# Layer 3's causal mask for the row maximum: added by VectorE in the operation that takes the maximum, in place of a matmul into the score bank

## The chip, the cores and the metric

One core of a Trainium2 chip runs the whole program. The metric is the device time of one execution in microseconds (us), the median of three runs: 2079.53 us before the change (2074.10 to 2083.88).

## The reference, cut to what matters

Four layers, each `x = x + attention(layernorm(x)) + feed_forward(layernorm(x))`, on 16 sequences of 256 tokens of 128 features. The change is in the attention of the last one:

```python
# layer 3: 16 heads of 8 features, T = 256 tokens
att = einsum('bhtd,bhsd->bhts', q, k) / sqrt(8)
att = att + (alibi + causal)          # causal: -inf where s > t, else 0
att = softmax(att, axis=-1)           # exp(att - max over s), divided by its sum
y = einsum('bhts,bhsd->bhtd', att, v)
x = x + y @ W_proj + b_proj + ffn(xn) # ffn: (silu(xn Wg) * (xn Wu)) Wd
```

The masked entries must not count for the row maximum, nor for the sum.

## The kernel before, in words

Layers are done one after the other. Within a layer the sequences are turns (-2 to 16), and `turn_steps` writes one list of steps a turn that TensorE (PE), VectorE (DVE), ScalarE (ACT) and SyncE (SP) all follow in its order. Turns 2 to 13 are a loop over two turns. Semaphores tie the engines; each instruction stream is in program order.

Attention of layer 3 needs two score matrices a head. In step S (`row_scores`, lines 531 to 541) a head's scores lie with queries on the partitions: queries 0 to 127 against keys 0 to 127 in bank columns 0 to 127, and queries 128 to 255 against all 256 keys in columns 128 to 383. DVE takes the two maxima from the bank (lines 1236 and 1237) into `mx`. In step M the maxima of 8 heads are transposed by PE (line 664) and subtracted from the extra rows of `stk` by DVE (line 1245), so that the second score matrix comes with the maximum taken off. In step T (`key_scores`, line 555) the scores are made again with keys on the partitions, ACT takes the exponential (line 804) and step O multiplies by the values (line 694).

Step S is one sequence ahead of step T. The list has T0 S1 H0 T1 S0 T2 S3 O3 M1 T3 S2 T4 S5 H1 J0 T5 S4 J1 T6 S7 O0 P0 T7 S6 Q0 P1 T8 S9 H2 Q1 V0 T9 S8 V1 T10 S11 O1 W0 M0 T11 S10 T12 S13 Y0 T13 S12 T14 S15 O2 T15 S14. (H and Y: the feed forward; J: divide by the sum; P and V: queries, keys and values of a later sequence; Q and W: the output projection.) Where a T is followed by an S, PE issues them as a pair: mask of T, waits for S's bank and operands, mask of S, then the four score matmuls (lines 665 to 674). The masks are matmuls of an identity with a bf16 mask (line 546 for T, line 528 for S), which start the bank with -1e30 above the diagonal; the scores are accumulated on them.

The steps S, M, P, V and J share the two banks of `pS` in turn: PE starts a use when DVE has freed the bank two uses before (`S_free`). Operands of S come from DRAM: SP stores the sequence that step W finished (line 1437, after a wait for W's vector operation), then packs queries and keys into DRAM with three transfers (line 1401), waits until they have landed, and spreads them over the partitions with one transfer for heads 0 to 7 and one for heads 8 to 15 (line 1412). S1 of the next turn waits for the first of these.

`tc.link` (line 239 is its wait) makes DVE wait for its own last operation; `settle` (line 224) is a semaphore increment of the engine by itself, with nothing waiting for it.

Of the kernel before, what the change touches and what calls it, by code (L numbers as in the profile page):

```python
# [17 lines left out]
BF16 = mybir.dt.bfloat16  # L18
I32 = mybir.dt.int32
U32 = mybir.dt.uint32  # L20
ALU = mybir.AluOpType
# [200 lines left out]
def settle(eng, sem):  # L222

    eng.sem_inc(sem, 1)
# [47 lines left out]
def build(nc, d, out):  # L272
    ctx = ExitStack()
    with ctx:
# [8 lines left out]
        def sem(name):  # L283
            if name not in sems:
# [55 lines left out]
        ident = sb("ident", [P, P])  # L340
        onesr = sb("onesr", [1, P])
        onesm = sb("onesm", [P, P])
        maskb = sb("maskb", [P, 2, P], BF16)
        identb = sb("identb", [P, P], BF16)
        rank = sb("rank", [P, NT, 16])
        neghalf = sb("neghalf", [P, NT])
# [63 lines left out]
            "ld_0": [(wr[0][:, :], d["wr0"]), (wq0[:, :, :], d["wq0"]), (bq0[:, :], d["bq0"]),  # L410
                     (bv0[:, :], d["bv0"].partition_broadcast(P))],
            "ld_cst": [(onesr[:, :], d["c_ones"][0:1, :]), (onesm[:, :], d["c_ones"]),
                       (maskb[:, :, :], d["c_mask"]), (identb[:, :], d["c_identb"]), (rank[:, :, :], d["c_rank"]),
                       (tri[:, :], d["c_tri"]), (rope0[:, :, :], d["c_rope0"]),
                       (rope2[:, :, :], d["c_rope2"]), (bitf[:, :], d["c_bitf"]), (blockno[:, :], d["c_blockno"])],
            "ld_1": [(wr[1][:, :], d["wr1"]), (br[1][:, :], d["br1"].partition_broadcast(P)),
# [54 lines left out]
        def _(pe):  # L471
# [50 lines left out]
            def head_rows(h):  # L522
                return slice(32 * (h % NG), 32 * (h % NG) + 32), h // NG

            def row_scores_mask(l, bank):

                if l == 3:
                    pe.matmul(bank.rearrange("p (c n) -> p c n", c=2)[:, :, 0:P], identb[:, :],
                              maskb[:, 0, None, :].to_broadcast([P, 2, P]), start=True, stop=True)

            def row_scores(l, side, h, bank, part):

                rows, j = head_rows(h)
                if l == 3:
                    c = 1 - part
                    o = bank[:, P:P + T] if c else bank[:, 0:P]
                    return pe.matmul(o, stk[rows, side, j, c * P:(c + 1) * P],  # L537
                                     stk[rows, side, j, T:T + (c + 1) * P],
                                     start=False, stop=True, skip_group_check=True)
                return pe.matmul(bank[:, part * T:(part + 1) * T], stk[rows, side, j, part * P:(part + 1) * P],  # L540
                                 stk[rows, side, j, T:2 * T], start=True, stop=True)

            def key_scores_mask(l, bank):

                if l == 3:
                    pe.matmul(bank.rearrange("p (c n) -> p c n", c=2)[:, :, 0:P], identb[:, :],
                              maskb[:, 1, None, :].to_broadcast([P, 2, P]), start=True, stop=True)

            def key_scores(l, side, h, bank, part):

# [9 lines left out]
            def take_turn(turn):  # L560
# [4 lines left out]
                for at, (kind, k, local) in enumerate(turn.steps):  # L565
# [73 lines left out]
                    elif kind == "P":  # L639
                        w = {0: wq0, 2: wq2, 3: wq3}[l]  # L640
                        for n, which in enumerate({0: [2 * k, 2 * k + 1]}.get(l, [k])):
                            ins = pe.matmul(bank[:, n * T:(n + 1) * T], w[:, which, :],  # L642
                                            XT[:, bass.ts(turn.row(2), T)], start=True, stop=True)
                        ins.then_inc(s("S_full"), 1)
                    elif kind == "V":
                        pe.wait_ge(s("row_staged"), PRIMED + turn.row(2))
                        w = {0: wq0[:, 4, :], 2: wq2[:, 2, :], 3: wq3[:, 2, :]}[l]
                        pe.matmul(bank[:, 0:P], xtb[:, nxt, k * P:(k + 1) * P], w, start=True, stop=True)\
                          .then_inc(s("S_full"), 1)
                    elif kind == "S":  # L650
                        if not paired:
                            pe.wait_ge(s("S_free"), PRIMED + use_s + local - 1)
                            row_scores_mask(l, bank)
                        pe.wait_ge(s(f"spread{k // 8}"), PRIMED + turn.count(16, 32))
                        if not paired:
                            row_scores(l, nxt, k, bank, 0)
                        row_scores(l, nxt, k, bank, 1).then_inc(s("S_full"), 1)
                        paired = False
                    elif kind == "M":

                        last = max(loc for kd, kk, loc in turn.steps[:at] if kd == "S") if k == 0 else -1
                        pe.wait_ge(s("S_free"), PRIMED + use_s + last + 1)
                        for n in range(4):
                            ins = pe.transpose(bank[:, n * P:(n + 1) * P], mx[:, n % 2, 2 * k + n // 2, :], ident[:, :])  # L664
                        ins.then_inc(s("S_full"), 1)
                    elif kind == "T":
                        if k < 8:
                            pe.wait_ge(s("S_free"), PRIMED + use_s - uses_behind_maxima(l, turn.n - 1))
                        else:
                            pe.wait_ge(s("S_free"), PRIMED + use_s + used_at(turn, "M", 1) + 1)  # L670
                        key_scores_mask(l, bank)
                        after = turn.steps[at + 1]
                        paired = after[0] == "S"
                        if paired:
                            other = pS[:, turn.s_bank(after[2]), :]
                            pe.wait_ge(s("S_free"), PRIMED + use_s + after[2] - 1)
                            pe.wait_ge(s(f"spread{after[1] // 8}"), PRIMED + turn.count(16, 32))
                            row_scores_mask(l, other)
                        key_scores(l, par, k, bank, 0)
                        if paired:  # L680
                            row_scores(l, nxt, after[1], other, 0)
                        key_scores(l, par, k, bank, 1).then_inc(s("T_full"), 1)
                    elif kind == "O":

                        back = 1 if k == NJ - 1 else 0
                        made = 0 if back else used_at(turn, "T", NG * k + NG - 1) + 1
                        pe.wait_ge(s("T_free"), PRIMED + use_t + made)
                        pe.wait_ge(s("v_ready"), PRIMED + turn.row(1 - back))
                        pe.wait_ge(s("O_free"), PRIMED + use_o + local)
                        for kc in range(2):  # L690
                            q0 = P if l == 3 and kc == 1 else 0
                            for g in range(NG):
                                h = NG * k + g
                                ins = pe.matmul(pO[32 * g:32 * g + DH + 1, q0:T],  # L694
                                                va[:, par ^ back, kc, h, :],
                                                pex[:, h % 8, kc * T:kc * T + T - q0],
                                                start=(kc == 0), stop=(kc == 1))
                        ins.then_inc(s("O_full"), 1)
                    elif kind == "J":

                        copied = [loc for kd, kk, loc in turn.steps if kd == "O" and kk == NJ - 1][0]
                        pe.wait_ge(s("O_free"), PRIMED + use_o + copied + 1)
                        for j in range(NJ):
                            ins = pe.transpose(bank[:, j * P:(j + 1) * P], oTf[:, j, k * P:(k + 1) * P], ident[:, :])
                        ins.then_inc(s("S_full"), 1)
                    elif kind == "Q":
                        pe.wait_ge(s("out_read"), PRIMED + turn.row())
                        pe.transpose(bank[:, 0:P], ob[:, k, :], ident[:, :]).then_inc(s("T_full"), 1)
                    elif kind == "W":
                        turned = [loc for kd, kk, loc in turn.steps if kd == "Q" and kk == 1][0]  # L710
                        pe.wait_ge(s("T_free"), PRIMED + use_t + turned + 1)
                        for c in range(2):
                            ins = pe.matmul(yb[:, c * P:(c + 1) * P], oT[:, c * P:(c + 1) * P], wp3[:, :],
                                            start=True, stop=True)
                        ins.then_inc(s("Y_full"), 1)
# [229 lines left out]
        def _(dve):  # L945
# [224 lines left out]
            def take_turn(turn, tc):  # L1170
# [17 lines left out]
                for kind, k, local in turn.steps:  # L1188
# [44 lines left out]
                    elif kind == "S":  # L1233
                        j, col = k // NG, 32 * (k % NG) + MAXROW
                        if l == 3:
                            dve.tensor_reduce(mx[:, 0, j, col:col + 1], bank[:, 0:P], AX.X, ALU.max)  # L1236
                            ins = dve.tensor_reduce(mx[:, 1, j, col:col + 1], bank[:, P:P + T], AX.X, ALU.max)  # L1237
                        else:
                            ins = dve.tensor_reduce(mx[:, :, j, col], bank.rearrange("p (c n) -> p c n", c=2),  # L1239
                                                    AX.X, ALU.max)  # L1240
# [225 lines left out]
def shape_constants():  # L1466
# [14 lines left out]
    fixed[:, 1, 1, 0], fixed[:, 1, 1, 1] = np.arange(T) / 256.0, -slope  # L1481
    c["c_fixed"] = fixed.reshape(P, 2, 2 * T)
    m = np.where(np.arange(P)[None, :] > np.arange(P)[:, None], -1e30, 0.0).astype(f)
    c["c_mask"] = np.stack([m, m.T], axis=1)
    c["c_identb"] = np.eye(P, dtype=f)
    freqs = (f(1.0) / np.power(f(10000.0), np.arange(0, DH, 2, dtype=f) / f(DH))).astype(f)
    ang = np.arange(T, dtype=f)[:, None] * freqs[None, :]
# [69 lines left out]
```

## Time and profile before

| | us |
|---|---|
| median of 3 runs | 2079.53 |
| the profiled execution, its own time | 2077.18 |
| its span | 2074.8 |
| layer 3's first maximum to the last | 1636.9 to 2047.8 |
| PE busy, whole span | 1624.0 |
| DVE busy, whole span | 1238.6 |
| ACT busy, whole span | 766.0 |

Times in the rows are us from the start of the span; a busy share is that of an engine whose instructions overlap at their ends. The granted clock (PEclk) is 1.00 for 2.4 GHz and 0.50 for 1.2 GHz.

### The profile page before, as it was taken

Reading aid. Unit: us, or ns where it says so; the run is one execution under the profiler, and the core shown is the slowest. Engines: PE = TensorE matmul, PEld = TensorE weight load, DVE = VectorE, ACT = ScalarE, POOL = GpSimd, SP = SyncE. Lnnn points to the kernel's source line nnn. Section 1 sums busy time; section 2 is a strip of 40 time slices with the busy share of each in tenths; the row PEclk is TensorE's granted clock in tenths of the full one; section 3 lists DMA queues with packets and bytes.
Section 4 is the critical chain, followed back from the end, with each engine's and each line's share of the span. In section 5 each row is a group of like instructions: output and inputs, shape, how many; then the busy total and the mean of one; then the engine's idle time right before and its main releaser. Section 6 shows DMA issues by size and latency. Waiting matters only on the chain.

```text
span 2074.8 us, 44343 instructions
## 1 busy us (share of the span) xinstructions
PE 1624.0 (78%) x12567; PEld 1050.6 (51%) x12567; DVE 1238.6 (60%) x3512; ACT 766.0 (37%) x1723; POOL 380.3 (18%) x488
## 2 busy tenths in 40 slices
PE   3257999999972599998983588888887688888888
PEld 3123666666632577877872244444543344444444
DVE  6454666566675665665574455555557566666664
ACT  2013445445441222322230254445454144434444
POOL 1274101101167011111123300000006200000000
PEclk9855999999965698988885598999997599999999
DMA  7023455455421000000001332333232111111110
GB/s 233 28 70 101 141 155 174 137 157 174 130 58 37 0 1 1 0 0 0 0 1 40 89 95 89 98 112 110 82 95 57 36 39 42 40 40 39 37 40 15
DMA packets 133278, 144.90 MB, mean 70 GB/s; under 512 B 15001, under 2 KB 114130, under 8 KB 132946
## 3 DMA queue, kind: packets, MB, share of 16 engines
q1 hardware_dynamic: 127058, 131.37, 21.4%
q0 software_dynamic: 6144, 12.60, 2.1%
q8 instruction: 38, 0.62, 0.1%
q14 instruction: 38, 0.31, 0.0%
HBM read 104.65 MB, written 39.52 MB: 69 GB/s over the span
## 4 chain that ended last, share of the span: by engine, by line
PE 48%; DVE 19%; issue 13%; DMA 8%; POOL 7%; SPq 2%; ACT 2%; DVEq 1%; ACTq 0%; POOLq 0%
PE pO L694 6%; DMA stk<-packed_qk 6%; PE pT_ L557 5%; PE pH L584 5%; PE pY L592 5%; DVE X L1278 4%; PE pH L500 4%; POOL sorted_x L910 3%; PE pS L642 3%; PE pS L664 3%; DVE mx L1239 2%; PE pT_ L490 2%; PE pY L512 2%; PE pT_ L555 2%; DVE stk L1245 2%
## 5 line engine op out<-in xcount | busy, mean ns | idle before, releaser
L804 ACT ACTIVATE pex<-pT_ 128x512 f32<-128x512 f32 (+1 forms) x768 | 426.6, 562 | 656.1 <-PE pT_ L557 362.8
L1239 DVE TENSOR_REDUCE mx<-pS 128x2 f32<-128x512 f32 x512 | 348.2, 688 | 194.9 <-PE pS L540 176.8
L557 PE MATMUL pT_<-stk 32*128 32x256 f16 x1024 | 208.2, 298 | 120.0 <-DMA stk<-packed_qk 67.0
L540 PE MATMUL pS<-stk 32*128 32x256 f16 x1024 | 220.3, 304 | 23.4 <-DMA stk<-packed_qk 19.6
L694 PE MATMUL pO<-pex,va 128*9 128x256 f32 (+1 forms) x3072 | 218.4, 408 | 2.0 <-ACT pex L804 2.0
L797 ACT ACTIVATE wb<-pH,b 128x256 f32<-128x256 f32 x256 | 107.3, 470 | 268.4 <-PE pH L500 268.4
L883 POOL TENSOR_TENSOR qk<-qkf,qk 128x512 f16<-128x512 f32 x48 | 55.4, 1155 | 779.5 <-DVE qk L1211 407.3
L557 PEld LDWEIGHTS pT_<-stk 32*128 32x128 f16 x1024 | 55.9, 94 | 238.0 <-issue 87.3
L500 PE MATMUL pH<-XT,w 128*128 (+1 forms) x512 | 146.7, 413 | 0.0
L584 PE MATMUL pH<-xsT,wb 128*128 128x128 f32 x888 | 134.1, 297 | 0.0
L1245 DVE SCALAR_TENSOR_TENSOR stk<-pS,stk 128x512 f16<-128x512 f32 x96 | 66.3, 691 | 109.2 <-PE pS L664 105.0
L592 PE MATMUL pY<-wb,hbs 128*128 128x128 f32 x888 | 128.5, 288 | 2.2 <-DVE ysb L1259 2.2
L584 PEld LDWEIGHTS pH<-xsT,wb 128*128 128x128 f32 x888 | 114.6, 202 | 23.2 <-issue 20.8
L807 ACT ACTIVATE xts<-pO 128x256 f32<-128x256 f32 x192 | 73.8, 384 | 130.6 <-PE pO L694 130.6
L592 PEld LDWEIGHTS pY<-wb,hbs 128*128 128x128 f32 x888 | 107.4, 191 | 26.5 <-issue 21.2
L694 PEld LDWEIGHTS pO<-pex,va 128*9 128x9 f32 x3072 | 68.9, 95 | 91.0 <-issue 41.5
L1236 DVE TENSOR_REDUCE mx<-pS 128x1 f32<-128x128 f32 x256 | 73.4, 287 | 60.5 <-PE pS L537 44.7
L642 PE MATMUL pS<-XT,wq 128*128 (+1 forms) x256 | 87.9, 452 | 26.1 <-issue 18.8
L1237 DVE TENSOR_REDUCE mx<-pS 128x1 f32<-128x256 f32 x256 | 105.8, 413 | 0.0
L500 PEld LDWEIGHTS pH<-XT,w 128*128 128x128 f32 x512 | 98.8, 212 | 10.2
L483 PE MATMUL pS<-ident,qkf 128*128 128x128 f32 x128 | 33.0, 429 | 86.9 <-DVE qkf L966 86.9
L910 POOL DMA_INDIRECT sorted_x<-XN,slot x96 | 92.9, 968 | 27.8 <-issue 26.7
(195 smaller groups left out, 2841.5 us busy)
## 6 DMA issues: line engine op xcount, KB each, us to landing
wb<-in_w SPq DMA_DIRECT2D x111, 514.0 KB, 3.8
stk<-packed_qk SPq DMA_DIRECT2D x96, 256.0 KB, 2.8
packed_qk<-qk SPq DMA_DIRECT2D x144, 128.0 KB, 2.0
xsb<-sorted_x SPq DMA_DIRECT2D x111, 64.0 KB, 3.4
sorted_y<-ysb SPq DMA_DIRECT2D x111, 64.0 KB, 3.1
sorted_x<-wb SPq DMA_DIRECT2D x2, 2048.0 KB, 13.3
w<-in_w SPq DMA_DIRECT2D x2, 1024.0 KB
out<-X SPq DMA_DIRECT2D x16, 128.0 KB, 1.8
```

Of the source, the lines that this page charges most:

```text
L500: ins = pe.matmul(bank[:, half * T:(half + 1) * T], w, XT[:, bass.ts(turn.row(), T)], start=True, stop=True)
L540: return pe.matmul(bank[:, part * T:(part + 1) * T], stk[rows, side, j, part * P:(part + 1) * P], stk[rows, side, j, T:2 * T], start=True, ...
L557: return pe.matmul(bank[:, part * T:(part + 1) * T], key, stk[rows, side, j, 0:T], start=True, stop=True)
L584: ins = pe.matmul(pH[:, local % 2, f * P:(f + 1) * P], wb[:, place_, f * P:(f + 1) * P], xsT[:, ring, :], start=True, stop=True)
L592: ins = pe.matmul(pY[:, 0:P], hbs[:, ring, f * P:(f + 1) * P], wb[:, place_, FF + f * P:FF + (f + 1) * P], start=(f == 0), stop=(f == NF - ...
L642: ins = pe.matmul(bank[:, n * T:(n + 1) * T], w[:, which, :], XT[:, bass.ts(turn.row(2), T)], start=True, stop=True)
L694: ins = pe.matmul(pO[32 * g:32 * g + DH + 1, q0:T], va[:, par ^ back, kc, h, :], pex[:, h % 8, kc * T:kc * T + T - q0], start=(kc == 0), s ...
L797: ins = act.activation(hb[:, k % 4, half * T:(half + 1) * T], bank[:, half * T:(half + 1) * T], ACT.Relu, bias=b1[1][:, 2 * k + half:2 * k ...
L804: act.activation(pex[:, k % 8, 0:n], bank[:, 0:n], ACT.Exp).then_inc(s("T_free"), 1)
L910: pool.indirect_dma_start(XS, bass.IndirectOffsetOnAxis(ap=slot[:, choice, t:t + 1], axis=0), XN[:, t, :], None).then_inc(sem("sorted_out" ...
L1239: ins = dve.tensor_reduce(mx[:, :, j, col], bank.rearrange("p (c n) -> p c n", c=2), AX.X, ALU.max)
L1245: dve.scalar_tensor_tensor(q, bank.rearrange("p (j n) -> p j n", j=2), -1.0, q, ALU.mult, ALU.add).then_inc(s("S_free"), 1)
```

## The change: what it does

The 256 mask matmuls of step S are gone (16 heads of 16 sequences); those of step T stay. The scores start their bank themselves. DVE's two maximum operations of a head become two `tensor_tensor_reduce`: each adds the bank (PSUM, f32) and a bf16 mask (SBUF), writes the sum to a new tile `masked` (SBUF, f32, nothing reads it) and writes its maximum to `mx`. Before the first of them stands a `settle`, behind the wait for the scores. The mask is laid out as 512 columns: mask, zeros, mask, and the mask of step T.

```diff
-            def row_scores_mask(l, bank):
-                if l == 3:
-                    pe.matmul(bank.rearrange("p (c n) -> p c n", c=2)[:, :, 0:P], identb[:, :],
-                              maskb[:, 0, None, :].to_broadcast([P, 2, P]), start=True, stop=True)
...
                     return pe.matmul(o, stk[rows, side, j, c * P:(c + 1) * P],
-                                     stk[rows, side, j, T:T + (c + 1) * P],
-                                     start=False, stop=True, skip_group_check=True)
+                                     stk[rows, side, j, T:T + (c + 1) * P], start=True, stop=True)
...
-                            row_scores_mask(l, bank)
...
-                            row_scores_mask(l, other)
...
                         if l == 3:
-                            dve.tensor_reduce(mx[:, 0, j, col:col + 1], bank[:, 0:P], AX.X, ALU.max)
-                            ins = dve.tensor_reduce(mx[:, 1, j, col:col + 1], bank[:, P:P + T], AX.X, ALU.max)
+                            settle(dve, sem("dve_settled"))
+                            for c, at in enumerate((slice(0, P), slice(P, P + T))):
+                                ins = dve.tensor_tensor_reduce(masked[:, turn.s_bank(local), at], bank[:, at],
+                                                               maskb[:, at], 1.0, -3e38, ALU.add, ALU.max,
+                                                               mx[:, c, j, col:col + 1])
...
-        maskb = sb("maskb", [P, 2, P], BF16)
+        maskb = sb("maskb", [P, 4 * P], BF16)
+        masked = sb("masked", [P, 2, 3 * P])
...
-    c["c_mask"] = np.stack([m, m.T], axis=1)
+    c["c_mask"] = np.concatenate([m, np.zeros((P, P), f), m, m.T], axis=1)
```

## Rows read from the trace of the kernel before

**Rows 1.** Stretch, length, busy (count): PE, PEld, DVE, ACT, POOL; clock, DMA, GB/s.

```profile
1863.00:1889.00 26.00, 21.82 (x210) 12.47 (x198) 17.00 (x52) 10.27 (x25) 1.50 (x2) 1.00 0.14 40
```

**Rows 2.** Chain of waits that ended last, one turn (start, length, what).

```profile
1836.31 2.59 DMA stk<-packed_qk
1843.92 0.28 PE pS L528
1848.27 0.28 PE pS L528
1856.05 0.28 PE pS L528
```

**Rows 3.** SP's transfers, timeline of the same turn.

```profile
1833.31 1.36 SPq L1401 DMA_DIRECT2D packed_qk<-qk  x3
1836.31 1.81 SPq L1412 DMA_DIRECT2D stk<-packed_qk  x2
```

**Rows 4.** PE, timeline of the same turn: two pairs of T and S.

```profile
1838.95 0.28 PE L528 MATMUL pS<-maskb,identb 128*128 128x256 bf16 x1 [1.00 <-DMA stk<-packed_qk]
1839.16 0.28 PE L555 MATMUL pT_<-stk 32*128 32x256 f16 x1
...
1840.40 0.27 PE L546 MATMUL pT_<-maskb,identb 128*128 128x256 bf16 x1
1840.51 0.27 PE L528 MATMUL pS<-maskb,identb 128*128 128x256 bf16 x1
```

**Rows 5.** DVE, timeline of the same turn.

```profile
1831.72 0.42 DVE L1332 TENSOR_TENSOR X<-X,pY 128x256 f32 x1 [0.76 <-PE pY L713]
...
1841.01 0.42 DVE L1286 SCALAR_TENSOR_TENSOR hbs<-hbs,pH 128x256 f32<-128x256 f32 x1 [0.82 <-ACT hbs L787]
1841.47 0.42 DVE L1288 SCALAR_TENSOR_TENSOR wb<-hbs,pH 128x256 f32<-128x256 f32 x1
...
1842.01 0.41 DVE L1237 TENSOR_REDUCE mx<-pS 128x1 f32<-128x256 f32 x1
1842.34 0.28 DVE L1236 TENSOR_REDUCE mx<-pS 128x1 f32<-128x128 f32 x1
...
1847.59 0.29 DVE L1236 TENSOR_REDUCE mx<-pS 128x1 f32<-128x128 f32 x1 [0.23 <-DVE ob L1322]
...
1849.76 0.41 DVE L1237 TENSOR_REDUCE mx<-pS 128x1 f32<-128x256 f32 x1
1850.44 0.48 DVE L1214 TENSOR_SCALAR qkf<-pS,bq 128x256 f32<-128x256 f32 x1 [0.27 <-PE pS L642]
...
1858.05 0.42 DVE L1332 TENSOR_TENSOR X<-X,pY 128x256 f32 x1 [0.76 <-PE pY L713]
```

**Rows 6.** Groups of instructions by line and form, 1700 to 1960 us.

```profile
L1237 DVE TENSOR_REDUCE mx<-pS 128x1 f32<-128x256 f32 x156 | 64.4, 413 | 0.0
L1236 DVE TENSOR_REDUCE mx<-pS 128x1 f32<-128x128 f32 x156 | 44.6, 286 | 34.9 <-PE pS L537 24.3 <-DVE ob L1322 2.3 <-DVE X L1328 2.2
...
L1223 DVE TENSOR_TENSOR va<-pS,bv 128x128 f32<-128x128 f32 x18 | 5.0, 281 | 0.0
...
L1269 DVE TENSOR_TENSOR X<-X,pY 128x256 f32 x9 | 3.8, 422 | 9.1 <-PE pY L518 9.1
```

**Rows 7.** DVE in layer 1: timeline, and two groups of tiny operations.

```profile
801.13 0.49 DVE L1299 BATCH_NORM_STATS2 zs<-pS 128x6 f32<-128x128 f32 x2 [2.57 <-PE pS L637]
801.77 0.25 DVE L1303 BATCH_NORM_AGGREGATE zmv<-zs 128x2 f32<-128x6 f32 x2
...
L1303 DVE BATCH_NORM_AGGREGATE zmv<-zs 128x2 f32<-128x6 f32 x26 | 3.2, 165 | 1.9
...
L1363 DVE TENSOR_SCALAR lam<-lamt 128x1 f32<-128x1 f32 x1 | 0.2, 154 | 0.2 <-DVE GA L1011 0.2
```

**Rows 8.** DVE, timeline of the first turn with S steps: every second head.

```profile
1638.44 0.29 DVE L1236 TENSOR_REDUCE mx<-pS 128x1 f32<-128x128 f32 x1 [0.17 <-PE pS L537]
...
1639.97 0.29 DVE L1236 TENSOR_REDUCE mx<-pS 128x1 f32<-128x128 f32 x1 [0.17 <-PE pS L537]
```

More of the change, by code:

```diff
@@ L412, in build @@
             "ld_cst": [(onesr[:, :], d["c_ones"][0:1, :]), (onesm[:, :], d["c_ones"]),
-                       (maskb[:, :, :], d["c_mask"]), (identb[:, :], d["c_identb"]), (rank[:, :, :], d["c_rank"]),
+                       (maskb[:, :], d["c_mask"]), (identb[:, :], d["c_identb"]), (rank[:, :, :], d["c_rank"]),
                        (tri[:, :], d["c_tri"]), (rope0[:, :, :], d["c_rope0"]),
@@ L546, in key_scores_mask @@
                     pe.matmul(bank.rearrange("p (c n) -> p c n", c=2)[:, :, 0:P], identb[:, :],
-                              maskb[:, 1, None, :].to_broadcast([P, 2, P]), start=True, stop=True)
+                              maskb[:, None, 3 * P:4 * P].to_broadcast([P, 2, P]), start=True, stop=True)
             def key_scores(l, side, h, bank, part):
```

## The prediction, made before the changed kernel was run

> **What bounds the kernel now.** I read the busy time by stretch first. W's vector operation comes every 26.33 us (1831.72, 1858.05 [rows 5]), which is a turn of layer 3; in 26.00 us of it PE is busy 21.82 us, DVE 17.00 us and ACT 10.27 us, at the full clock (1.00) [rows 1]. No engine is full, so the turn must be a loop of hand-overs, and I went to the chain of waits, then to the timelines of SP, PE and DVE. Two parts close the loop. I cut them at the transfer that brings heads 0 to 7.
>
> Part B is a chain of transfers. Step W's vector operation starts at 1831.72 and ends at 1832.14 [rows 5]; SP stores, then packs from 1833.31, and spreads at 1836.31, when the packed rows have landed [rows 3]; that spread lands at 1838.90 [rows 2], and S1 starts at once, after PE has idled 1.00 us for it [rows 4]. Fixed: 6.8 us from W's end, whatever PE and DVE do in it. Five of the 16 heads (T11 to T15 with their S) run in its shadow.
>
> Part A runs from there (1838.95) to the next W (1858.05) [rows 4, 5], 19.1 us with the other 11 heads. PE's order sets most of it, but PE hands to DVE and back. The chain of waits goes through S mask matmuls at 1843.92, 1848.27 and 1856.05, which waited for DVE to free a bank [rows 2]; what freed it were maxima and M's vector operation. So the same head's step is on the path both as PE's mask and as DVE's maximum. The reader is to see that a saving counts only in part A, and that the change takes from PE and gives to DVE inside one loop.
>
> **What is removed.** Where PE only follows its order, a mask costs the step from L546 to L528, 1840.40 to 1840.51: 0.11 us. Where PE waits for a bank or a transfer ahead of it, the mask of T has long run, and what goes is the whole step from L528 to the scores, 1838.95 to 1839.16: 0.21 us [rows 4]. In part A the path goes through four masks of the second kind (1838.95, and the three of the chain) and one of the first (T8 with S9, behind P1): 4 x 0.21 + 0.11 = 0.95 us a turn. The other masks of part A are beside work of DVE or ACT that ends later; they are worth nothing unless that work shrinks. Those of part B only lengthen PE's idle 1.00 us. Over the span 256 masks at 0.11 us would be 28 us of PE; I count about half of that on the path.
>
> **What is added, per head.** I call the growth of DVE's pair of operations a.
> - The streams. A two-source operation on PSUM takes 281 ns for 128 columns and 422 ns for 256, against 286 and 413 ns for the maxima [rows 6]. Growth: 0.00 to 0.01 us; I take none. The extra output `masked` goes to SBUF with nobody waiting.
> - The maximum as a second output. No operation of this trace has two outputs. From below: it rides along, and a is 0.01. From above: each becomes a tiny operation of its own that starts only when the main one has ended: that loses the overlap of about 0.08 us (a maximum starts at 1842.34, 0.33 us behind one of 0.41 [rows 5]) and adds one of 154 ns [rows 7], so 0.23 each, a = 0.46. Between: a tiny operation queued directly behind. Two aggregations of 128x2 take 0.25 us together and one 0.165 [rows 7], so the second adds 0.085; twice, a = 0.17. I take 0.17, since these are the rows of a tiny result behind another operation with no wait.
> - The Trainium skill, "VectorE: DVE Perf Modes", section "Two Vector instructions with no wait between them", says that an operation that also writes out its accumulator is two instructions, the main one and an accumulator read. No run here shows it yet. It speaks against the change, and for the middle or upper bound. By the 75 ns per overlapped instruction in its "Vector Engine (DVE) Microarchitecture Reference" (5.2), a would be an estimated 0.15.
> - The settle, s. Behind a wait for its own statistics and a settle, DVE's aggregation starts at 801.77, 0.15 us after 801.62 [rows 7]; a maximum after a plain own wait and one increment (1847.59) shows 0.23 us of idle [rows 5]. A bare own wait takes about 0.04 (1841.43 to 1841.47 [rows 5]). So one more increment is about 0.12 us where DVE is idle or has just waited for itself, and none where it is busy with another operation and the increment passes meanwhile. The sequencer does run ahead: maxima follow each other at 0.33 us [rows 5]. Bounds 0 and 0.15; I take 0.12 for heads S4, S7 and S8, which stand behind own waits of J0, J1 and V0, and 0 for S0 and S6. What is queued behind the settle on DVE is the rest of the list, J, P, V and M among it, and PE waits for these by `S_free`.
>
> **The sum for part A.** Shift of each hand-over against before, in us:
> - S1's scores -0.21; H0, S0's maximum and M1 follow: -0.21 + a. Mask of S5 gone behind M's vector operation: -0.42 + a. H1 and J0 likewise. S4: -0.42 + 2a + s.
> - Two ways to P0's vector operation. Through PE (S7's scores without mask, O0, P0): -0.63 + 2a + s. Through DVE (J1, S7's maximum): S7's maximum ends at about 1850.09 in overlap terms (1849.76 + 0.33) and P0 starts at 1850.44 [rows 5]: 0.35 us, of which 0.03 is a hand-over and 0.32 slack: -0.42 - 0.32 + 3a + 2s = -0.74 + 3a + 2s.
> - With a = 0.17, s = 0.12 these are -0.17 and +0.01; DVE is the later: +0.01. P1 waits for P0: +0.01. T8 with S9: -0.10. H2, V0 the same. S8: -0.10 + 0.17 + 0.12 = +0.19. S11's scores without mask: -0.02. O1, W: -0.02.
>
> In closed form the turn moves by -0.70 + 4a (at s = 0.12), zero at a = 0.175: the gain of PE and the price of DVE cancel. In part B DVE has 5 x (0.17 + 0.12) = 1.45 us more, but its waits there are for PE, and PE has the idle 1.00 us and 5 x 0.11 of masks: hidden. If that cover went, each further 0.1 us would be 0.1 a turn. S and T steps overlap in turns 0 to 14: 15 x -0.02 = -0.3 us.
>
> The first turn has S without T. Two heads take 1.53 us there (1638.44 to 1639.97), 0.77 each, PE-paced: DVE idles 0.17 us before each second head [rows 8]. Without the mask DVE paces, at its pair's 0.54 us (286 and 413 ns [rows 6], each less the overlap of 0.08) + 0.17 = 0.71: -0.06 over perhaps 10 heads, -0.6 us; with settles exposed, +0.5. I take 0. Layers 0 to 2 are untouched; the mask's load, 512 columns in place of 256, lies among the loads of the start, far ahead of layer 3.
>
> Sum: 2077.2 - 0.3 = 2076.9 us against the profiled execution's 2077.18. The median of the runs shown is 2.35 us above that, so I forecast 2079.
>
> **The rivals.** Half a per cent of the time, 10.4 us, is about what a measurement of this kernel tells from none.
> - Slow result (slower). The maximum is written by an operation that waits for the main one's end. Place: S0, S4, S7 and S8 of part A, between DVE and PE. Decides from a = 0.345. At a = 0.46: -0.70 + 1.84 = +1.14 us a turn, +17 us: 2097; at a = 0.35, 2090. For: nothing in the trace writes two results. Against: small operations overlap. Chance 0.23.
> - Free result (faster). a = 0.01: -0.66 us a turn, -10 us: 2069; with the settle hidden as well (s = 0) -1.0, -15 us: 2064. For: the vector engine has gaps of 9 us a turn, and the sequencer runs ahead. Against: the settle follows own waits. Chance 0.14.
> - Half rate (slower). An operation with two sources and two results goes one column in two clocks: 384 columns more at the rate of 128 in 0.127 us (413 - 286 ns [rows 6]) are 0.38 us, a = 0.55 with the tiny results: +1.5 a turn, 2102. The Trainium skill's "Vector Engine (DVE) Microarchitecture Reference" (section 7) has such halving for two SBUF sources that are not bf16; here one is PSUM and the other bf16, so by it none is due. Chance 0.06.
> - That the masks were not on the path at all (the change does for PE nothing that counts): then only DVE's side is left, 2a to 4a a turn less what slack takes, +5 to +10 us: 2087. The chain of waits speaks against it. Chance 0.07.
>
> The forecast (a from 0.10 to 0.30, 2073 to 2087 us) has 0.50. **Numbers.** Faster by over 0.5% takes 0.12 (most of the free result), slower 0.23 (the slow result above 2090, half rate), within 0.5% the rest, 0.65. The range is 2068 to 2097: from the free result to the slow one at a = 0.46.
>
> **What would show it.** Lines 528's groups gone and PE's busy time down by 256 x 0.28 us in the records; scores directly behind T's mask at about 0.2 us; after a wait, at once. On DVE two operations of about 0.29 and 0.42 us a head and perhaps two tiny ones; the start of the next operation behind the pair 0.17 us later than now; 0.34 in place of 0.23 us of idle behind J and V. PE's idle time for the spread at the turn's start should grow from 1.00 to about 1.5 us, and the period of the turns stay at 26.3 to 26.5 us. Wrong would be a period off by 0.3 us or more, a pair of over 1 us, or PE's wait for the spread shrinking to nothing, which would mean that DVE paces part B too.

## The result and the profile after

| | before | changed |
|---|---|---|
| median of 4 runs, us | 2078.12 | 2097.82 |
| the profiled execution, its own time | 2077.18 | 2093.68 |
| layer 3, first maximum to last | 1636.9 to 2047.8 | 1633.8 to 2064.7 |

Ratio of the changed kernel to the one before: 1.010, 95% interval 1.0053 to 1.0148. In a second comparison (e5) it was 1.0134 (1.0069 to 1.0199). Slower, by about 20 us, and 20 us is what layer 3 is longer by in the profile (410.9 to 430.8 us). The prediction said 2079, range 2068 to 2097.

The operations first, in the groups by line and form of the changed kernel, 1700 to 1960 us (they answer to [rows 6]):

```profile
L1230 DVE CUSTOM_DVE_ANT_0 masked<-pS,maskb 128x256 f32<-128x256 f32 x150 | 62.9, 419 | 0.0
L1230 DVE CUSTOM_DVE_ANT_0 masked<-pS,maskb 128x128 f32<-128x128 f32 x150 | 43.1, 287 | 37.9 <-PE pS L532 25.5 <-DVE va L1215 3.5 <-DVE ob L1317 3.5
...
L1230 DVE DVE_READ_ACCUMULATOR2_ANT mx<- 128x1 f32 x300 | 24.8, 83 | 0.1
```

The main operations take 287 and 419 ns, where the plain maxima took 286 and 413. Each has a second, tiny instruction that reads the accumulator, 83 ns. What it costs its engine shows in the timeline of VectorE, changed kernel (it answers to [rows 5]):

```profile
1829.94 0.29 DVE L1230 CUSTOM_DVE_ANT_0 masked<-pS,maskb 128x128 f32<-128x128 f32 x1 [0.38 <-DVE ob L1317]
...
1844.69 0.42 DVE L1230 CUSTOM_DVE_ANT_0 masked<-pS,maskb 128x256 f32<-128x256 f32 x1
1845.04 0.08 DVE L1230 DVE_READ_ACCUMULATOR2_ANT mx<- 128x1 f32 x1
1845.04 0.28 DVE L1230 CUSTOM_DVE_ANT_0 masked<-pS,maskb 128x128 f32<-128x128 f32 x1
1845.25 0.08 DVE L1230 DVE_READ_ACCUMULATOR2_ANT mx<- 128x1 f32 x1
1845.25 0.42 DVE L1230 CUSTOM_DVE_ANT_0 masked<-pS,maskb 128x256 f32<-128x256 f32 x1
```

The read and the next main operation start together (1845.04, 1845.25). Behind the operation of 256 columns the next one starts after 0.35 us, where it was 0.33. So a, the growth of a head's pair of operations, is 0.02 to 0.03 us, not 0.17. The first operation behind a wait of VectorE for its own last one starts after 0.38 us of idle, where it was 0.23: 0.15 more.

So VectorE's side came out cheap, and the kernel is slower all the same. The busy time by stretch, from the store of turn 0 to that of turn 13 (13 turns), tells why. Each row gives the stretch, its length, the busy time (and count) of PE, PEld, DVE, ACT and POOL, the mean granted clock and the DMA share and rate; before above, changed below:

```profile
1697.60:2042.10 344.50, 292.07 (x2780) 165.93 (x2779) 226.95 (x685) 141.22 (x325) 17.95 (x24) 1.00 0.14 40
```

```profile
1696.50:2059.40 362.90, 297.86 (x2574) 166.12 (x2570) 231.92 (x1101) 141.12 (x325) 17.95 (x24) 0.87 0.13 38
```

PE has 206 matmuls fewer and is busy for longer, since its mean granted clock is 0.87 in place of 1.00. The clock has two levels in these rows, 0.50 (1.2 GHz) and 1.00 (2.4 GHz), so 0.87 means 0.13 x 2 x 362.9 = 94 us at the low one. The trace's own records of the clock say 92 us, and 3.4 us for the kernel before. A piece of a low stretch in turn 0, in which PE has no idle time at all, and then four whole turns from store to store, changed kernel:

```profile
1708.00:1712.00 4.00, 4.00 (x31) 1.67 (x31) 2.60 (x11) 1.51 (x4) 0.00 (x0) 0.50 0.00 0
...
1841.01:1866.99 25.98, 20.06 (x199) 11.50 (x198) 17.84 (x86) 10.83 (x25) 1.50 (x2) 1.00 0.14 40
1759.48:1786.10 26.62, 22.74 (x205) 13.03 (x203) 18.05 (x86) 10.83 (x26) 1.50 (x2) 0.90 0.14 40
2004.65:2030.18 25.53, 20.13 (x202) 11.51 (x198) 17.91 (x85) 10.87 (x25) 1.50 (x2) 1.00 0.14 41
1730.63:1759.48 28.85, 23.65 (x199) 13.19 (x198) 17.98 (x85) 10.88 (x25) 1.50 (x2) 0.85 0.13 38
```

The turns at 1.00 take 25.98 and 25.53 us; the one at 0.85 takes 28.85. A turn of the kernel before:

```profile
1832.57:1858.84 26.27, 22.35 (x216) 12.77 (x214) 17.50 (x54) 10.86 (x25) 1.50 (x2) 1.00 0.14 40
```

Against the same turns before (26.28 and 26.09 us) the change is a gain of 0.3 to 0.6 us a turn where the clock is full. At full clock PE is now busy 20.1 us of a turn, where it was 22.4. PE's timeline, changed kernel, shows the start of a low stretch, which the clock's records put at 1792.07, for 6.8 us:

```profile
1790.65 0.28 PE L540 MATMUL pT_<-maskb,identb 128*128 128x256 bf16 x1
1792.52 0.39 PE L549 MATMUL pT_<-stk 32*128 32x256 f16 x1 [1.59 <-DMA stk<-packed_qk]
...
1792.95 2.08 PE L501 MATMUL pH<-XT,wf 128*128 x4
```

PE waits 1.59 us for the spread (1.00 before [rows 4]; I had said 1.5). The clock falls within this wait, and the four matmuls that follow take 2.08 us. In the kernel before the same four took 1.13:

```profile
1839.43 1.13 PE L500 MATMUL pH<-XT,wf 128*128 x4
```

### The profile page after: what moved, and what is told of

It reads as the page before. It is cut to its first block, busy times and chain, and to the rows that moved or that the text cites. A ratio compares the mean times of both kernels' runs of the same rounds, so it can differ in the third digit from the quotient of the medians.

```text
span 2091.6 us, 44614 instructions
## 1 busy us (share of the span) xinstructions
PE 1631.5 (78%) x12311; PEld 1049.9 (50%) x12311; DVE 1244.1 (59%) x4024; ACT 766.2 (37%) x1723; POOL 381.2 (18%) x488
## 4 chain that ended last, share of the span: by engine, by line
PE 48%; DVE 19%; issue 14%; DMA 7%; POOL 7%; SPq 2%; ACT 1%; DVEq 1%; ACTq 0%; POOLq 0%
PE pO L686 6%; PE pT_ L551 5%; PE pH L578 5%; DMA stk<-packed_qk 5%; PE pY L586 5%; PE pH L501 5%; DVE X L1273 4%; POOL sorted_x L902 3%; PE pS L657 3%; PE pS L636 3%; DVE mx L1234 3%; PE pT_ L549 2%; PE pT_ L491 2%; PE pY L513 2%; POOL XN L922 1%
## 5 line engine op out<-in xcount | busy, mean ns | idle before, releaser
L686 PE MATMUL pO<-pex,va 128*9 128x256 f32 (+1 forms) x3072 | 226.2, 420 | 2.0 <-ACT pex L796 2.0
L1230 DVE CUSTOM_DVE_ANT_0 masked<-pS,maskb 128x128 f32<-128x128 f32 (+1 forms) x512 | 159.3, 353 | 65.2 <-PE pS L532 45.0
L549 PE MATMUL pT_<-stk 32*128 32x256 f16 (+1 forms) x512 | 93.5, 266 | 36.0 <-DMA stk<-packed_qk 18.1
L586 PEld LDWEIGHTS pY<-wb,hbs 128*128 128x128 f32 x888 | 107.4, 191 | 26.5 <-issue 21.2
L532 PE MATMUL pS<-stk 32*128 32x256 f16 (+1 forms) x512 | 95.8, 273 | 10.6 <-DMA stk<-packed_qk 8.2
```

The lines of the kernel that those rows point to most:

```text
L549: return pe.matmul(bank[:, part * T:part * T + T - q0], key, stk[rows, side, j, q0:T], start=False, stop=True, skip_group_check=True)
L586: ins = pe.matmul(pY[:, 0:P], hbs[:, ring, f * P:(f + 1) * P], wb[:, place_, FF + f * P:FF + (f + 1) * P], start=(f == 0), stop=(f == NF - ...
L686: ins = pe.matmul(pO[32 * g:32 * g + DH + 1, q0:T], va[:, par ^ back, kc, h, :], pex[:, h % 8, kc * T:kc * T + T - q0], start=(kc == 0), s ...
L1230: ins = dve.tensor_tensor_reduce(masked[:, turn.s_bank(local), at], bank[:, at], maskb[:, at], 1.0, -3e38, ALU.add, ALU.max, mx[:, c, j, c ...
```

## The experiments

Two theories stood after the result. Clock theory: the step itself gains, but with less work TensorE is granted the low clock in stretches of layer 3. VectorE theory: the slowdown is the price of the pair of operations and the settle, and the clock has no part in it. Several experiments add idle matmuls: repeats of T's own mask matmul (256 columns) into the same bank, which leave the same values there. The columns of the table: the ratio to the kernel before with its interval; the time from the store of turn 0 to that of turn 13 in the profiled run; and the time at 1.2 GHz in it, summed from the clock's records. Whole times differ between the groups of runs: the kernel before took 2195 us beside e1 to e4, 2190 beside e13 and 2078 to 2079 beside the rest. It is not the chip alone, since e5 to e8 and e13 ran on one chip. In e1 to e4 and e13 the last exponential of layer 0, where nothing was changed, comes 83 to 92 us later than in the profile of the kernel before. So only ratios are compared, and the 13 turns.

| | PE in step S | VectorE | idle matmuls a turn | ratio | 13 turns | us low |
|---|---|---|---|---|---|---|
| before | masks | plain | 0 | 1 | 344.6 | 3 |
| e8, before again | masks | plain | 0 | | 343.9 | 3 |
| changed | none | new | 0 | 1.010 (1.005, 1.015) | 362.9 | 92 |
| e5, changed again | none | new | 0 | 1.013 (1.007, 1.020) | 361.0 | 92 |
| e1 | masks | new | 0 | 1.006 (1.004, 1.009) | 351.6 | 14 |
| e2 | none | plain | 0 | 1.001 (0.998, 1.004) | 358.9 | 92 |
| e3 | none | new | 16, ahead of S's wait | 0.998 (0.995, 1.000) | 338.7 | 3 |
| e10, e3 again | none | new | 16, same | 0.9975 (0.9959, 0.9991) | 345.3 | 17 |
| e4 | none | new | 10, T0 | 1.004 (1.001, 1.007) | 349.3 | 36 |
| e6 | none | plain | 16, as e3 | 0.994 (0.991, 0.997) | 334.7 | 7 |
| e7 | masks | plain, settle | 0 | 1.006 (1.004, 1.008) | 347.6 | 3 |
| e9 | none | new | 24, six waits | 0.998 (0.9965, 0.9994) | 338.0 | 0 |
| e12 | none | new | 8, every second T | 1.007 (1.004, 1.009) | 363.2 | 65 |
| e13 | none | new | 16 of 128 columns | 1.002 (1.000, 1.005) | 343.8 | 20 |

The profiled run is one draw. Those of the changed kernel and e5 were the fastest of their four, e2's was the slowest of its ten (2187 to 2212 us), e10's the slowest of its nine, with its 17 us low in the first two turns. e12 has 41 of its 65 us in the first three turns. So the time at the low clock is good for tens of us, not for single ones.

**e1, the masks put back, VectorE as changed.**

```diff
+                            row_scores_mask(l, bank)
...
+                            row_scores_mask(l, other)
```

> The changed kernel with the 256 mask matmuls of step S put back where they were (the scores that follow overwrite them): TensorE's work is that of the kernel before, VectorE's that of the changed one. Clock theory (the changed kernel loses its time to stretches at 1.2 GHz in layer 3, because TensorE has less to do): granted clock 1.00 in turns 1 to 13 as before, time 2078 to 2088 (the settle's 0.15 us at three places of a turn, 15 turns, is up to 7 us). VectorE theory (the pair of operations and the settle cost the time): 2098 or more, since the masks' time is added again and nothing of VectorE's is taken away.

The clock is 0.98, with 14 us low in four short stretches in place of 92. The ratio is 1.006, between what the two theories had said (at most 1.005, at least 1.009). VectorE's side has a price then: the 13 turns are 7 to 8 us longer than before, of which about 3 go with the 10 us more at the low clock (at the 0.27 us each found below), and turns at full clock take 26.8 to 27.1 us. But putting 256 matmuls back made the 13 turns 11 us shorter than in the changed kernel:

```profile
1811.60:2163.20 351.60, 297.16 (x2780) 169.64 (x2782) 232.80 (x1101) 141.24 (x325) 17.94 (x24) 0.98 0.14 39
```

**e2, PE as changed, VectorE as before.** The maximum is taken without the mask, and the exponential is scaled to keep it finite, so this kernel does not compute the reference; each engine's work is that of the comparison.

```diff
-                                     stk[rows, side, j, T:T + (c + 1) * P],
-                                     start=False, stop=True, skip_group_check=True)
+                                     stk[rows, side, j, T:T + (c + 1) * P], start=True, stop=True)
...
-                            row_scores_mask(l, bank)
...
-                            row_scores_mask(l, other)
...
-                        act.activation(pex[:, k % 8, 0:n], bank[:, 0:n], ACT.Exp).then_inc(s("T_free"), 1)
+                        act.activation(pex[:, k % 8, 0:n], bank[:, 0:n], ACT.Exp, scale=1e-3 if l == 3 else 1.0)\
+                            .then_inc(s("T_free"), 1)
```

> TensorE without the masks of step S as in the changed kernel, VectorE with the two plain maxima of the kernel before, and no settle. The maximum is taken over unmasked scores, and the exponential's scale is 0.001 to keep it finite: the numbers are not the reference's, the work of each engine is. Clock theory: stretches at 1.2 GHz in layer 3 as in the changed kernel, time 2085 to 2100, no faster than before although 256 matmuls are gone and nothing is added. VectorE theory: 0.95 us a turn are gained and nothing is paid, 2062 to 2067, at the full clock.

Nothing was added, 256 matmuls were taken away, and it is no faster (1.001). The clock is at 0.87 as in the changed kernel:

```profile
1818.60:2177.50 358.90, 297.26 (x2574) 165.02 (x2570) 225.62 (x685) 141.31 (x325) 17.94 (x24) 0.87 0.13 38
```

The VectorE theory falls here: its 2062 to 2067 was a ratio of 0.992 to 0.995, at the full clock. The clock theory had the clock right and the time somewhat too high: its 2085 to 2100 is 1.003 to 1.010. The 14 us that e2's 13 turns are longer than before are those of its slowest run; its median is 11 us below that.

**e3, an idle matmul ahead of each wait.**

```diff
                         key_scores_mask(l, bank)
+                        if turn.steps[at + 1][0] == "S":
+                            for _ in range(1):
+                                key_scores_mask(l, bank)
```

> The changed kernel, and in every step T that is followed by an S a second, idle copy of T's own mask matmul (256 columns, bf16, same bank), ahead of the wait for S's bank. TensorE does as many matmuls as before the change, but the added one runs while it waits where it waits. Clock theory: clock 1.00, and a turn 0.3 to 0.5 us shorter than before (0.21 less at each of three or four waits, 0.15 more at three settles): 2070 to 2076. VectorE theory: 2098 or more.

```profile
1814.40:2153.10 338.70, 284.26 (x2780) 163.11 (x2782) 231.84 (x1101) 141.48 (x325) 17.96 (x24) 0.99 0.14 41
```

As the clock theory had it: as many matmuls as before, 8 us less busy PE time, most turns 25.8 to 26.2 us. Against the changed kernel, matmuls were added on the engine that is fullest, and the 13 turns are 24 us shorter.

**e4, ten idle matmuls in front of the spread only.**

```diff
+                        if k == 0:
+                            for _ in range(10):
+                                key_scores_mask(l, bank)
```

> The changed kernel with ten more copies of T0's mask matmul (1.07 us at full clock) in front of the wait for the transfer of heads 0 to 7, where TensorE idles 1.6 to 1.9 us a turn. If the clock falls because of this one long idle stretch: clock 1.00 throughout and 2067 to 2072, since nothing else is lengthened. If it falls because of the mean work of a turn (0.11 x 16 = 1.8 us missing): some low stretches stay, 2075 to 2092. VectorE theory: unchanged, 2094 to 2100.

36 us low, 1.004: between the changed kernel and the one before. Ten matmuls in the longest wait give a part of the clock back, not the whole. Since 16 were removed, this does not tell too few from the wrong place.

**e5, the changed kernel again, and e8, the kernel before again.**

> The changed kernel again, beside the others of this call. Clock theory: ratio to the kernel before 1.005 to 1.012, some ten stretches of 3 to 17 us at 1.2 GHz among the turns of layer 3, and about 26.0 us from store to store in turns without such a stretch.

> The kernel before, unedited, for its profile on the same chip as the others: turns of 26.3 to 26.6 us at clock 1.00, at most two low stretches in turns 2 to 14, by either theory.

92 us low against 3, as in the first pair, so the first comparison was not a chance draw. e5's ratio of 1.013 is slightly above its range. e8 is a single run.

**e6, e2 with the idle matmuls of e3.**

> As e2 (no masks in step S, plain maxima, exponential's scale 0.001, so not the reference's numbers), and in every step T that is followed by an S one idle copy of T's mask matmul ahead of the wait for S's bank. Against e2 it only adds 240 matmuls. Clock theory: it is nevertheless faster than e2 by 10 us or more, at clock 1.00 in the turns, 25.4 to 25.8 us each, 0.992 to 0.996 of the kernel before. If the low stretches cost nothing, or come from something else: as e2 or slower by up to 0.11 us x 16 a turn.

```profile
1696.00:2030.70 334.70, 284.85 (x2781) 163.45 (x2782) 225.40 (x685) 141.49 (x325) 17.94 (x24) 0.99 0.14 41
```

Against e2 it only adds matmuls: 24 us less in the 13 turns, most turns 25.5 to 25.8 us, and a ratio of 0.994 against 1.001. This is the cleanest pair of the study, since VectorE's program is the old one in both; each ratio is to the kernel before beside it. Against the kernel before, e6 has as many matmuls, moved from behind a wait to ahead of it. That is worth (344.6 - 334.7) / 13 = 0.76 us a turn (0.71 with e8's 343.9).

**e7, the settle alone.**

```diff
+                            settle(dve, sem("dve_settled"))
                             dve.tensor_reduce(mx[:, 0, j, col:col + 1], bank[:, 0:P], AX.X, ALU.max)
```

> The kernel before with nothing but the settle added ahead of the two plain maxima. It prices the settle: exposed at three hand-overs of a turn, 0.15 us each, it would be 0.3 to 0.45 us a turn (turns of 26.8 us in place of 26.4), +5 to +7 us, ratio 1.002 to 1.003, at clock 1.00. If the pair of operations itself is what costs VectorE's side, 26.4 us a turn as before.

In the 13 turns it costs 3.0 to 3.7 us (against the two profiles of the kernel before), 0.23 to 0.29 a turn. Its first operation behind J's own wait shows 0.34 us of idle:

```profile
1803.60 0.29 DVE L1237 TENSOR_REDUCE mx<-pS 128x1 f32<-128x128 f32 x1 [0.34 <-DVE ob L1323]
```

That is 0.11 above the kernel before; the new operation adds the other 0.04 of the 0.38. The ratio, 1.006 (some 12 us), is above the 1.003 at most that had been expected, and more than the 13 turns show. In the profile the last exponential of layer 0, where nothing was changed, comes 8 to 10 us later than in the two profiles of the kernel before, but it does so by 5 to 6 us in e10 too, whose median is low. That rest is not explained, and e1's 1.006 may hold the same.

**e9, idle matmuls only where PE waits, and e10, e3 again.**

```diff
+                        for _ in range({0: 10, 4: 3, 6: 2, 7: 2, 10: 3, 12: 4}.get(k, 0) if l == 3 else 0):
+                            key_scores_mask(l, bank)
```

> The changed kernel with 24 idle copies of T's mask matmul a turn, placed only in the six steps T behind which TensorE waits (T0: 10, T4: 3, T6: 2, T7: 2, T10: 3, T12: 4), so that they lie in idle time. Clock theory: clock 1.00 as in e3, and turns of 25.8 to 26.0 us, no longer than e3's: ratio to the kernel before 0.993 to 0.998. If what counts is that work is spread evenly over the turn (steps 13 to 15 and 1 to 3 get none here): some low stretches, 0.998 to 1.004.

> e3 again (one idle copy ahead of each wait) in more rounds, beside e9. Clock theory: 0.995 to 0.999 of the kernel before, turns of 26.0 us, at most 7 us at 1.2 GHz over turns 0 to 13. VectorE theory is out by e2 and e6; a ratio of 1.000 or more would mean that the 0.4 us a turn seen in e3's profile don't reach the time.

```profile
1699.40:2037.40 338.00, 293.81 (x2886) 176.35 (x2882) 230.86 (x1101) 140.54 (x325) 17.93 (x24) 1.00 0.14 41
```

No low stretch at all in e9, and most turns 25.9 to 26.3 us; e10 has 17 us low, where at most 7 had been expected. Both beat the kernel before with their intervals clear of 1, by 4 to 5 us (2074.05 and 2074.68 against 2078.76), and the changed kernel, by its ratio, by over 20.

**e12 and e13, half the added columns, in half or all of the instructions.**

```diff
+                        if turn.steps[at + 1][0] == "S" and k % 2 == 0:
+                            for _ in range(1):
+                                key_scores_mask(l, bank)
...
+                        if l == 3 and turn.steps[at + 1][0] == "S":
+                            pe.matmul(bank[:, 0:P], identb[:, :], maskb[:, 3 * P:4 * P], start=True, stop=True)
```

The first edit is e12's, the second e13's, which stands ahead of T's mask and is overwritten by it. e11, named in the first text, is the form of e13 with the idle matmul behind T's mask; it gave no time.

> As e3, with a 256-column copy in every second step T only: half of e3's columns a turn in half of the instructions. If columns over some stretch count, as e11: 10 to 60 us at 1.2 GHz, 1.000 to 1.006. If the number of instructions counts, more low stretches than e11.

> As e3, but the idle matmul of each step T has 128 columns in place of 256, and stands ahead of T's mask: as many instructions as in e3, half of the columns, as e12 has. If the matmuls' columns keep the clock up: as e12 (65 us at 1.2 GHz between the stores of turns 0 and 13, ratio 1.007), or between it and e3. If the number of instructions, or the gap ahead of each wait, counts: as e3, 3 to 17 us at 1.2 GHz, 0.997.

With the same added columns, e12 had 65 us low and a ratio of 1.007 (1.004, 1.009), e13 20 us and 1.002 (1.000, 1.005). So the time comes back by degrees: with half of e3's columns both ratios stay above e3's and e10's 0.998, clear of their intervals. The two ratios hint that columns alone do not decide and that those spread over all pairs hold the clock up better, but the intervals touch, there is one profile each, and e3 and e10, the same kernel, differ by 14 us low. Whether columns, instructions or gaps decide is open.

## Why the prediction was wrong

- **The loop, parts A and B.** Right at full clock: there the turn moved by what part A gives, and PE's wait for the spread grew from 1.00 to 1.59 us, as said for part B.
- **The masks' price at full clock.** Said: 0.95 us a turn, of which 4 x 0.21 = 0.84 stood behind waits. e6, which keeps an idle matmul in each pair, can show only that part: 0.71 to 0.76, with 7 us of low clock in it. Right in kind, perhaps somewhat high; the 0.11 of the fifth mask has no run.
- **The second result (a).** Said 0.17 a head, chosen between 0.01 and 0.46; measured 0.02 to 0.03. The Trainium skill's "VectorE: DVE Perf Modes", section "Two Vector instructions with no wait between them", was right that there are two instructions; the trace adds that the second, of 83 ns, starts together with the next main operation and takes it almost nothing. 128 columns more cost the main operation 132 ns (287 to 419), where they cost the plain maximum 127, so there is no halving either.
- **The settle (s).** Said 0.12 behind own waits; 0.11 by itself (e7), 0.15 with the new operation. Right.
- **A sign that was wrong from the start.** PE's busy time was to fall by 256 x 0.28 = 72 us. The records overlap, so at full clock it fell by 2.3 us a turn, 0.14 for each mask; over the whole span it rose, from 1624.0 to 1631.5 us, since what is left runs slower.
- With a = 0.025 and s = 0.15 the closed form of the text, -1.06 + 4a + 3s, gives -0.51 us a turn. e9, at full clock throughout, measures (338.0 - 344.6) / 13 = -0.51, or -0.45 with e8's 343.9; e3 gives -0.45. That the second decimals meet is luck; that the form holds to 0.1 us is not. Over 15 turns it is -8 us: with its own terms put right and the clock held, the forecast would have been 2071, near the "free result" rival.
- **Luck.** The sum's a was too large by 0.58 us a turn (4 x 0.145), 9 us in all, and this error brought the forecast nearer to the measured time. The "slow result" rival's 2097 meets the measured 2097.82, but its cause, a of 0.46, is not there.
- **The step that failed.** "at the full clock (1.00)": the text read the granted clock of the kernel before as a condition, carried every row at 2.4 GHz into the changed kernel and gave the clock no rival and no chance. Taking 16 matmuls out of each turn took PE from 22.4 to 20.1 us of work in 26, and that was enough: 92 us of the 13 turns ran at 1.2 GHz, and the turns took 27.9 us on average, where 26.3 to 26.5 had been said. From e3 to the changed kernel that is 24.2 us for 89 us more at the low clock, 0.27 us each; from e6 to e2 it is 24.2 us for 85, 0.28 each. -0.5 x 13 for the steps and 0.28 x 89 for the clock make +18.4 for the 13 turns, which are 18.3 us longer in the profiles. The medians say +19.7.
- The rows that could have warned were there: in 26.00 us PE was busy 21.82 us [rows 1] and kept 1.00, while it had 0.50 elsewhere. The page of the kernel before has PE's busy share and clock in 40 slices, in tenths:

```profile
PE   3257999999972599998983588888887688888888
PEclk9855999999965698988885598999997599999999
```

  The six slices at 5 have PE busy 2 to 7, among them the start of layer 3 (the 32nd, 6); where PE has 8 or 9, the clock is 7 or more. It is no strict rule: the first two slices have 3 and 2 at a clock of 9 and 8.
- The Trainium skill's "TensorE: Matmul & The Clock Gate", Part 1, says that the chip grants the full clock by how busy the array has been and that the low one is the default. By that rule a removal of TensorE's work is a risk for the work that stays, and the trace agrees: 3 us low before, 92 after.

## What to carry to other kernels

Before taking matmuls from an engine that waits in each turn for others, look at the granted clock, and price the case in which it falls: what is gained at full clock can be lost again on the work that is left, as 24 us were here. Matmuls put where TensorE waits anyway cost little and can hold the clock up (e9: 24 idle ones a turn, the 13 turns 23 to 25 us shorter than in the two profiles without; the changed kernel's two turns at full clock, 25.99 and 25.53 us, are 25.90 and 25.56 there). A measured gain or loss of a removal is that of the step only if the clock's row is the same on both sides.

## What the runs showed of the hardware that was not expected

- The maximum that a two-source operation writes out comes from a second instruction of 83 ns. It starts together with the next operation, and a pair of them takes 0.02 to 0.03 us of the engine's pace.
- A removal of 206 matmuls of 2780 in 345 us took the mean granted clock from 1.00 to 0.87, in the changed kernel twice and in e2. As many idle ones, elsewhere in the turn, brought it back to 0.98 or 0.99 (e3, e10, e6), half of them to 0.91 (e12).
- A semaphore increment that VectorE makes by itself, behind a wait for its own last operation, delays the next operation by 0.11 us: 3.0 to 3.7 us over 13 turns.
